# GNN and mixture-of-experts kernel on one Trainium2 core: the first expert stage finishes and normalises its own rows

## The chip, the cores and the metric

The kernel is one program on one NeuronCore of a Trainium2 chip. The metric is the device time of one execution in microseconds (us), the median of three runs. TensorE (PE in the profile; PEld is its weight loading), VectorE (DVE), ScalarE (ACT), GpSimd (POOL) and SyncE (SP) each run their own instruction stream. They meet only in semaphores. All transfers are issued by SP, ACT or POOL and run on the core's 16 DMA engines.

## The reference

The input is a graph of 3125 nodes with 256 features and 53125 edges. Two layers follow one another, each a graph part and a feed-forward part with experts. Around the change stands this:

```python
x = x + _L0_gnn_ref(_layernorm(x), ...)                  # attention over the edges
x = x + _L0_ffn_ref(_layernorm(x)[None], ...)[0]         # one of 8 experts a node
#   H = gelu(xf @ W1 + b1); probs = softmax(H @ Wg + bg); e = argmax(probs)
#   out = probs[e] * (H @ Wd[e] + bd[e])
x = x + _L1_gnn_ref(_layernorm(x), W1, W2, b, src, dst)
#   feat = _layernorm(x); out_deg = how often a node is a source, at least 1
#   msg = (feat @ W1)[src] + (feat[src] * feat[dst]) @ W2
#   msg = msg / (sqrt(out_deg[src]) * sqrt(out_deg[dst])); agg = segment_sum(msg, dst)
x = x + _L1_ffn_ref(...)                                 # two of 8 experts a node
```

All sums over `src` in the second graph part are linear in `feat[src] / sqrt(out_deg[src])`. The kernel therefore gathers rows of the normalised x, scaled by the root of the degree, and calls them f.

## The kernel before, in words

The program is a row of blocks. In each block every engine has its own list of instructions, and all engines meet at the block's end. Nodes stand in T = 25 tiles of P = 125 rows, five tiles to a group (G = 5, NG = 5). `x_sb` is x in SBUF, `n_sb` the normalised x.

**Attention update (lines 1178 to 1390).** For each group VectorE adds the projected attention to `x_sb`, normalises it and keeps it in `n_sb`. SP stores `x_sb` to the DRAM tensor `sum0` (line 1205) and `n_sb` to `tok0` (line 1208). VectorE also works out `rsq_deg`, the inverse root of the out-degree (line 1265), after the first group.

**Routing `route("r0", ...)`.** Every node picks one expert; nodes are sorted into NB0 = 32 blocks of S = 128 rows, each of one expert. `from_i`, `to_i` and `gate_i` hold, column by column, the node rows that a block reads, the rows that it writes (unfilled slots go to 256 spare rows behind the nodes) and its gate values.

**First expert stage `experts("m0", ...)`.** All 32 blocks pass through it in turns of two slots. The second expert stage `m1` (56 blocks) uses the same function with `own_w1` true.
- SP: `load_w2` waits for `s_ye`, then loads the block's 1 MB second weight (line 1660) and its bias (line 1661), into one of two slots.
- POOL: for block b it issues `load_rows(b + 3)`, an indirect gather of 128 rows from `tok0` (line 1678); `add_rows(b)`, which waits for the finished rows and for the store before and then scatters them into `sum0` with an add on the way (line 1693); and `load_gates(b + 2)` (line 1684).
- PE, in a loop over turns: hidden(b + 1), 32 matmuls (line 1739); turn(b + 2), two transposes (line 1728); output(b), 16 matmuls (line 1762).
- ACT: the gelu of the hidden values.
- DVE, for block b: `fetch_rows` copies the turned rows of block b + 2 from PSUM (line 1805), which the hidden product of that block waits for. Then `fetch_output(b)` waits for the output, adds the bias (line 1819), releases `s_ye`, waits for the gate and multiplies by it (line 1823).

`dve_order.link` (line 62 in the trace) makes an instruction raise a semaphore on which the next one of the same engine waits. In a loop each such wait takes its value from a register, for which a small register instruction is issued. `v.sem_inc(carrier, 1)` carries one wait more.

**Load, normalise, store (lines 1849 to 1935).** After the experts: SP loads all of `sum0` into `x_sb` (line 1904); VectorE takes mean and variance of each row (lines 1870, 1873), an inverse root by a shift and three Newton steps (`inverse_root`, lines 162 to 167, eleven instructions), and ScalarE (line 1895) and VectorE (line 1886) write f into `yt`; SP stores it to `f_rows` (line 1908) and waits for the store.

**Edge sums (lines 1940 to 2116).** For 84 groups of 5 edge columns, POOL gathers the rows f[src] from `f_rows`, 381 gathers (line 1969; it runs up to GI = 4 groups ahead of VectorE). 39 more columns are made by TensorE instead (line 1989), from one-hot matrices (line 2015) and `f_part`, f split into three bf16 parts; for these SP first loads f back in five chunks (line 2110). VectorE adds up runs (line 2027), ACT keeps the sums (line 2099), SP stores them (line 2115). In groups 3 to 27 VectorE also writes one tile of `n_sb` each (line 2052), for the stage behind.

Of the kernel before, what the change touches and what calls it, by code (L numbers as in the profile page):

```python
# [8 lines left out]
ALU = mybir.AluOpType  # L9
# [62 lines left out]
def build(nc, x, src, dst, edge_attr_64, L0_gnn_Wq, L0_gnn_Wk, L0_gnn_Wv, L0_gnn_We, L0_gnn_Wo, L0_gnn_bo,  # L72
# [22 lines left out]
    with top:  # L95
# [8 lines left out]
        f_rows = dram("f_rows", [N_NODES, D])  # L104
# [4 lines left out]
        sum0 = dram("sum0", [N_NODES + 2 * S, D])  # L109
# [1070 lines left out]
        s_lgT, s_res, s_fold = sem2("logits_turned"), sem2("residual_ready"), sem2("fold_made")  # L1180
        s_tok = [sem(f"tokens{n}_stored") for n in range(2)]
        s_base = [sem(f"residual{n}_stored") for n in range(2)]
        HALF = (313, 312)
        with ExitStack() as st:
# [13 lines left out]
            @block.sync  # L1198
            def _(sp):
                for n, rows in enumerate((sum0, sum1)):  # L1200
                    sp.dma_start(rows[N_NODES:N_NODES + 2 * S], x[0:2 * S]).then_inc(s_base[n], 16)
                with sp.Fori(0, NG) as i:
                    sp.wait_ge(s_kept3, i + 1)
                    for a, b in HALVES:
                        sp.dma_start(rows_of_tiles(sum0[0:N_NODES])[a:b, bass.ds(i * G, G), :], x_sb[a:b, bass.ds(i * G, G), :])\
# [14 lines left out]
            def _(v):  # L1220
# [44 lines left out]
                inverse_root(v, rsq_deg[:], degree[:], root_t[:, 0:T])  # L1265
                for i in range(2, NG):
# [125 lines left out]
        v_ctx.close()  # L1392

# [219 lines left out]

        def experts(name, n_blocks, tok, s_tok, total, s_base, W1, W2, b2, own_w1):
# [8 lines left out]
            with ExitStack() as st:  # L1623
# [7 lines left out]
                yr = [sb(st, f"{name}yr_{n}", [S, D]) for n in range(2)]  # L1631
# [6 lines left out]
                s_yg, s_gate = sem(name + "_y_weighed"), [sem(f"{name}_gate{n}_loaded") for n in range(2)]  # L1638
                block = st.enter_context(nc.Block(no_gpsimd_drain=True))
# [34 lines left out]
                def _(pool):  # L1674
# [12 lines left out]

                    def add_rows(b):
# [12 lines left out]
                    pool.wait_ge(s_base, 32 * NG + 16)  # L1701
                    for b in range(n_blocks):
# [86 lines left out]
                def _(v):  # L1789
# [34 lines left out]

                    v.sem_inc(s_ye, 2)
                    for s in range(2):
                        fetch_rows(0, s, slice(s, s + 1))
                    for s in range(2):
                        fetch_rows(1, s, slice(s + 2, s + 3))
                        fetch_output(0, s, slot_used=False)  # L1830
                    with v.Fori(1, turns - 1) as t:
                        dve_order.turn(t - 1, 4 if own_w1 else 2)
                        for s in range(2):
                            fetch_rows(t + 1, s, bass.ds(t * 2 + s + 2, 1))
                            fetch_output(t, s)
                    dve_order.leave(turns - 2)
                    for s in range(2):
                        fetch_output(turns - 1, s)
# [4 lines left out]
        experts("m0", NB0, tok0, s_tok[0], sum0, s_base[0], L0_ffn_W1, L0_ffn_Wd, L0_ffn_bd, False)  # L1843
# [5 lines left out]
        s_mv6, s_f6, s_f6d, s_f6st = sem("moments6_ready"), sem("f6_ready"), sem("f6_last_ready"), sem("f6_stored")  # L1849
        n6_ctx = ExitStack()  # L1850
        mv6 = sb(n6_ctx, "mv6", [P, T, 2])
        inv_dev6 = sb(n6_ctx, "inv_dev6", [P, T])
        with ExitStack() as st:
            yt = sb(st, "yt6", [P, T, D])
            stats6 = sb(st, "stats6", [P, T, 6])
            sq6 = sb(st, "sq6", [P, T])
            scale6 = sb(st, "scale6", [P, T])
            shift6 = sb(st, "shift6", [P, T])
            block = st.enter_context(nc.Block(no_gpsimd_drain=True))
            PARTS6 = (slice(0, 3), slice(3, NG))  # L1860

            @block.vector
            def _(v):
                link = lambda ins: dve_order.link(v, ins)

                def moments(i):

                    v.wait_ge(s_sum[i], 32)
                    for t in range(i * G, (i + 1) * G):
                        last = nc.vector.bn_stats(stats6[:, t, :], x_sb[:, t, :])  # L1870
                    link(last)
                    for t in range(i * G, (i + 1) * G):
                        last = nc.vector.bn_aggr(mv6[:, t, :], stats6[:, t, :])
                    link(last)

                for part in PARTS6:
                    for i in range(part.start, part.stop):
                        moments(i)
                    tiles = slice(part.start * G, part.stop * G)
                    link(nc.vector.tensor_scalar(sq6[:, tiles], mv6[:, tiles, 1], LN_EPS, None, ALU.add))  # L1880
                    inverse_root(v, inv_dev6[:, tiles], sq6[:, tiles], root_t[:, tiles])
                    link(nc.vector.tensor_tensor(scale6[:, tiles], inv_dev6[:, tiles], rsq_deg[:, tiles], ALU.mult))
                    nc.vector.scalar_tensor_tensor(shift6[:, tiles], mv6[:, tiles, 0], -1.0, scale6[:, tiles], ALU.mult, ALU.mult)\
                      .then_inc(s_mv6, 1)
                for t in range((NG - 1) * G, T):
                    last = nc.vector.tensor_scalar(yt[:, t, :], x_sb[:, t, :], mv6[:, t, 0:1], scale6[:, t:t + 1],
# [605 lines left out]
```

## Time and profile before

| | us |
|---|---|
| median of 3 runs | 2324.05 |
| lowest and highest | 2320.11, 2327.67 |
| the profiled execution's own time | 2315.66 |
| its span, first to last instruction | 2313.9 |

| stage | from, to in the profiled span (us) |
|---|---|
| attention update | about 734, 875 |
| routing | 875, 926 |
| first expert stage | 926, 1175 |
| load, normalise, store | 1175, 1207 |
| edge sums | 1207, 1697 |
| second graph part, routing | 1697, 1876 |
| second expert stage, output | 1876, 2314 |

In the profile, busy times are sums over a whole run or a window. "Idle before <-releaser" is how long the engine stood before an instruction, and what ended it. A DMA's "us to landing" runs from the issue's start to its semaphore.

### The profile page before, as it was taken

The numbers are of one execution on the slowest core, as the hardware profiler recorded it, in microseconds if no ns is written. First come the engines' busy times: TensorE is split into PE (matmuls) and PEld (weight loads), VectorE is DVE, ScalarE is ACT, GpSimd is POOL, SyncE is SP. The second block draws the span as 40 slices with busy tenths as digits, with TensorE's granted clock in tenths as the row PEclk, the third lists the DMA queues.
The fourth block names the chain that finished last, engine by engine and source line by source line (L and its number), as shares of the span: only waits on it lengthen the run. The fifth ranks groups of instructions, "written<-read, shape, count | busy, mean of one in ns | idle before, by whom it ended". The sixth has DMA issues, their size and how long they took to land. (4 is left out here: it accounts for less than half of the span.)

```text
span 2313.9 us, 39305 instructions
## 1 busy us (share of the span) xinstructions
PE 1788.1 (77%) x12108; PEld 1523.0 (66%) x12109; DVE 1236.2 (53%) x2537; ACT 909.2 (39%) x1928; POOL 1179.8 (51%) x1175
## 2 busy tenths in 40 slices
PE   5627987878864896899912888788868459999996
PEld 4415766666654674899912777677647459999996
DVE  6527977777778532111137887777737742222221
ACT  4415765555531343344424222222224243333442
POOL 1575777777741200444417777777750024444443
PEclk9858987787776898899965998989979569999998
DMA  5387655555564110676767766666640467777775
GB/s 124 100 186 170 171 155 154 154 155 155 152 155 100 46 45 23 191 199 199 200 167 208 237 219 219 219 220 230 223 143 23 143 211 198 198 198 196 198 199 147
DMA packets 224088, 383.62 MB, mean 166 GB/s; under 512 B 38181, under 2 KB 167748, under 8 KB 223764
## 3 DMA queue, kind: packets, MB, share of 16 engines
q1 hardware_dynamic: 158988, 243.83, 34.6%
q0 software_dynamic: 64160, 136.38, 23.4%
q10 hardware_dynamic: 840, 2.16, 0.3%
q8 instruction: 52, 0.85, 0.2%
q14 instruction: 48, 0.39, 0.1%
HBM read 287.62 MB, written 98.35 MB: 167 GB/s over the span
## 5 line engine op out<-in xcount | busy, mean ns | idle before, releaser
L790 POOL DMA_INDIRECT qr<-q_rows,src_t x405 | 396.2, 978 | 140.3 <-issue 120.3
L1969 POOL DMA_INDIRECT fr<-f_rows,src_i x381 | 360.6, 946 | 155.1 <-issue 112.7
L1989 PE MATMUL psP<-f_part,onehot 125*128 125x256 bf16 x2925 | 359.3, 287 | 80.3 <-DVE onehot L2015 80.3
L1989 PEld LDWEIGHTS psP<-f_part,onehot 125*128 125x128 bf16 x2925 | 298.2, 103 | 134.7 <-DVE onehot L2015 88.1
L884 PE MATMUL psK<-kp,oh_k 126*128 x1680 | 285.0, 327 | 92.0 <-DVE qr L967 55.2
L884 PEld LDWEIGHTS psK<-kp,oh_k 126*128 126x128 bf16 x1680 | 189.8, 113 | 182.5 <-issue 107.4
L2027 DVE SCALAR_TENSOR_TENSOR psA<-psA,same,fr 128x256 f32<-128x256 f32 x420 | 206.5, 492 | 89.7 <-DMA fr<-f_rows,src_i 57.7
L2099 ACT ACTIVATE acc<-psA 128x1280 f32<-128x1280 f32 x84 | 103.9, 1237 | 327.5 <-DVEq L2030 318.4
L1719 ACT ACTIVATE m1hT<-m1psH,m1par 128x128 f32<-128x128 f32 x448 | 128.1, 368 | 250.2 <-PE m1psH L1739 250.2
L1739 PEld LDWEIGHTS m1psH<-m1xT,m1w 128*128 128x128 f32 x1792 | 210.7, 193 | 2.8
L1739 PE MATMUL m1psH<-m1xT,m1w 128*128 128x128 f32 x1792 | 210.9, 276 | 0.0
L1762 PE MATMUL m1psY<-w_all,m1hT 128*128 x896 | 203.4, 380 | 0.0
L967 DVE TENSOR_TENSOR qr<-qr,psK 128x512 f32<-128x512 f32 (+1 forms) x252 | 136.1, 592 | 103.9 <-DMA qr<-q_rows,src_t 101.8
L1693 POOL DMA_INDIRECT sum<-m1yr,to_i x56 | 89.6, 1600 | 188.0 <-DVE m1yr L1823 185.1
L1762 PEld LDWEIGHTS m1psY<-w_all,m1hT 128*128 128x128 f32 x896 | 165.9, 190 | 21.2
L811 ACT ACTIVATE dist<-loc,k_neg 126x640 bf16<-126x640 bf16 x170 | 130.8, 819 | 67.2 <-DMA loc<-locals_ 38.5
L2015 DVE TENSOR_TENSOR onehot<-psP,node_f 125x3200 bf16<-125x3200 f32 x39 | 136.1, 3489 | 10.0 <-PE psP L1980 6.8
L1719 ACT ACTIVATE m0hT<-m0psH,b 128x128 f32<-128x128 f32 x256 | 73.2, 369 | 142.2 <-PE m0psH L1739 142.2
L970 DVE TENSOR_REDUCE dots<-qr 128x40 f32<-128x1280 f32 x84 | 125.0, 1488 | 2.9
L1739 PEld LDWEIGHTS m0psH<-m0xT,m0w 128*128 128x128 f32 x1024 | 120.6, 194 | 1.6
L1739 PE MATMUL m0psH<-m0xT,m0w 128*128 128x128 f32 x1024 | 120.7, 277 | 0.0
L815 ACT ACTIVATE oh_k<-dist,ones 126x1280 bf16<-126x1280 bf16 x85 | 115.8, 1362 | 10.1
(479 smaller groups left out, 2678.3 us busy)
## 6 DMA issues: line engine op xcount, KB each, us to landing
m1w<-in_L_ffn_W_dram SPq DMA_DIRECT2D x56, 1024.0 KB
run_rows<-acc SPq DMA_DIRECT2D x84, 640.0 KB
m0w<-in_L_ffn_Wd_dram SPq DMA_DIRECT2D x32, 1024.0 KB, 5.4
loc<-locals_ SPq DMA_DIRECT2D x85, 157.5 KB
ea<-in_edge_attr_dram SPq DMA_DIRECT2D x84, 140.0 KB
w_all<-in_L_ffn_W_dram SPq DMA_DIRECT2D x8, 1024.0 KB
m1b<-in_L_ffn_b_dram SPq DMA_DIRECT2D x56, 128.0 KB, 2.9
qr<-q_rows,src_t POOLq DMA_INDIRECT x420
```

Of the source, the lines that this page charges most:

```text
L790: nc.gpsimd.indirect_dma_start(out=qr[:, n % GQ, u, :], out_offset=None, in_=q_rows, in_offset=bass.IndirectOffsetOnAxis(ap=src_t[:, n, u: ...
L811: last = nc.scalar.activation(dist[:, c - CD, :], loc[:, slot, :], ACT.Abs, bias=k_neg[:, c:c + 1])
L884: last = nc.tensor.matmul(psK[:, m, (u - a) * D:(u - a + 1) * D], oh_k[:, K_SLOT[g], c, u * E:(u + 1) * E], kp[:, bass.ds(first[u] + c, 1) ...
L967: nc.vector.tensor_tensor(row[:, a:b].rearrange("p u d -> p (u d)"), row[:, a:b].rearrange("p u d -> p (u d)"), psK[:, m, 0:(b - a) * D], ...
L970: nc.vector.tensor_reduce(dots[:, :, at].rearrange("p h u -> p u h"), row.rearrange("p u (h d) -> p u h d", h=H), AX.X, ALU.add).then_inc( ...
L1719: last = nc.scalar.activation(hT[s][:, m, :], psH[s][:, m * 128:(m + 1) * 128], ACT.Gelu, bias=par[s][:, m:m + 1] if own_w1 else b1_0[:, m ...
L1739: last = nc.tensor.matmul(psH[s][:, m * 128:(m + 1) * 128], w1[s if own_w1 else 0][:, k, m * 128:(m + 1) * 128], xT[s][:, k, :], start=(k ...
L1762: last = nc.tensor.matmul(psY[:, s, 0:D], hT[s][:, m, :], w, start=(m == 0), stop=(m == KC - 1))
L1969: nc.gpsimd.indirect_dma_start(out=fr[:, n % GI, u, :], out_offset=None, in_=f_rows, in_offset=bass.IndirectOffsetOnAxis(ap=src_i[:, n * G ...
L1989: last = nc.tensor.matmul(psP[:, k % 2, 0:D], onehot[:, k % 2, t, :], f_part[:, c, t, :], start=(t == 0 and c == 0), stop=(t == T - 1 and ...
L2015: nc.vector.tensor_tensor(onehot[:, k % 2], psP[0:P, k % 2, D:D + E].unsqueeze(1).to_broadcast([P, T, E]), node_f[:].unsqueeze(2).to_broad ...
L2027: link(nc.vector.scalar_tensor_tensor(sums(n, u), prev, same[:, n * G + u:n * G + u + 1], fr[:, n % GI, u, :], ALU.mult, ALU.add))
```

## The change

Each block of the first expert stage now also gathers its residual rows, with the degree's root as a 257th column, from `base0`. VectorE finishes x, normalises it, scales it, and POOL scatters x and f side by side as 2 KB rows to `pair_rows`, without an add. The block that loaded, normalised and stored is gone. The edge sums gather f from `pair_rows` at index 2*src + 1 (`f_at`), load x behind group 12, take its moments in groups 24 to 48 and write `n_sb` in groups 50 to 74. In the attention update `base0` takes the place of `sum0`, and one more store writes its last column.

```diff
-        f_rows = dram("f_rows", [N_NODES, D])
-        sum0 = dram("sum0", [N_NODES + 2 * S, D])
+        base0 = dram("base0", [N_NODES, D + 1])
+        pair_rows = dram("pair_rows", [N_NODES + 2 * S, 2 * D])
...
-                for n, rows in enumerate((sum0, sum1)):
-                    sp.dma_start(rows[N_NODES:N_NODES + 2 * S], x[0:2 * S]).then_inc(s_base[n], 16)
+                sp.dma_start(sum1[N_NODES:N_NODES + 2 * S], x[0:2 * S]).then_inc(s_base[1], 16)
+                sp.wait_ge(s_root3, 1)
+                sp.dma_start(rows_of_tiles(base0[:, D:D + 1]), rsq_deg[:].unsqueeze(2), allow_slow_non_contiguous=True).then_inc(s_base[0], 16)
...
+                    def load_base(b):
+                        if b >= 2:
+                            pool.wait_ge(s_yst[b % 2], 16 * (b // 2))
+                        nc.gpsimd.indirect_dma_start(out=yr[b % 2][:, 0:D + 1], out_offset=None, in_=base0,
+                                                     in_offset=bass.IndirectOffsetOnAxis(ap=from_i[:, b:b + 1], axis=0))\
+                          .then_inc(s_xb[b % 2], 16)
+                    def store_pairs(b):
+                        pool.wait_ge(s_yg, b + 1)
+                        nc.gpsimd.indirect_dma_start(out=total, out_offset=bass.IndirectOffsetOnAxis(ap=to_i[:, b:b + 1], axis=0),
+                                                     in_=yr[b % 2][:], in_offset=None).then_inc(s_yst[b % 2], 16)
...
                         if b + 3 < n_blocks:
                             load_rows(b + 3)
-                        add_rows(b)
+                        if own_w1:
+                            add_rows(b)
+                        else:
+                            if b + 1 < n_blocks:
+                                load_base(b + 1)
+                            store_pairs(b)
                         if b + 2 < n_blocks:
                             load_gates(b + 2)
...
+                    def finish_rows(t, s):
+                        b = t * 2 + s
+                        link = lambda ins: dve_order.link(v, ins)
+                        rows, mean, var = yr[s][:, 0:D], y_mean[:, 0:1], y_root[:, 0:1]
+                        v.wait_ge(s_y, b + 1)
+                        v.sem_inc(carrier, 1)
+                        link(nc.vector.tensor_tensor(y_own[:], psY[:, s, 0:D], b2r[s][:], ALU.add))
+                        v.sem_inc(s_ye, 1)
+                        v.wait_ge(s_gate[s], (t + 1) * 16)
+                        v.sem_inc(carrier, 1)
+                        v.wait_ge(s_xb[s], (t + 1) * 16)
+                        v.sem_inc(carrier, 1)
+                        link(nc.vector.scalar_tensor_tensor(rows, y_own[:], gate_s[s][:, 0:1], rows, ALU.mult, ALU.add))
+                        v.sem_inc(carrier, 1)
+                        link(nc.vector.bn_stats(y_stats[:], rows))
+                        v.sem_inc(carrier, 1)
+                        link(nc.vector.bn_aggr(y_mean[:], y_stats[:]))
+                        link(nc.vector.tensor_scalar(var, y_mean[:, 1:2], LN_EPS, None, ALU.add))
+                        inverse_root(v, y_root[:, 1:2], var, y_root[:, 2:3])
+                        link(nc.vector.tensor_tensor(y_root[:, 1:2], y_root[:, 1:2], yr[s][:, D:D + 1], ALU.mult))
+                        nc.vector.tensor_scalar(yr[s][:, D:2 * D], rows, mean, y_root[:, 1:2], ALU.subtract, ALU.mult).then_inc(s_yg, 1)
...
-        with ExitStack() as st:
-            yt = sb(st, "yt6", [P, T, D])
...
-                sp.wait_ge(s_f6st, 32 * NG)
+        f_rows = pair_rows.rearrange("n (a d) -> (n a) d", a=2)
...
+        MOMENTS = 24
+        NORMS = MOMENTS + T + 1
...
-                    if 3 <= n < 3 + T:
-                        t = n - 3
+                    if MOMENTS <= n < MOMENTS + T:
+                        t = n - MOMENTS
+                        if t % G == 0:
+                            v.wait_ge(s_sum[t // G], 32)
+                            v.sem_inc(carrier, 1)
+                        link(nc.vector.bn_stats(stats6[:, t, :], x_sb[:, t, :]))
+                        link(nc.vector.bn_aggr(mv6[:, t, :], stats6[:, t, :]))
+                    if n == MOMENTS + T:
+                        link(nc.vector.tensor_scalar(var6[:], mv6[:, :, 1], LN_EPS, None, ALU.add))
+                        inverse_root(v, inv_dev6[:], var6[:], root_t[:, 0:T])
+                        link(nc.vector.tensor_tensor(inv_dev6[:], inv_dev6[:], has_in[:], ALU.mult))
+                    if NORMS <= n < NORMS + T:
+                        t = n - NORMS
...
                 for n in range(NK):
+                    if n >= MOMENTS // 2 and n % 2 == 0 and (n - MOMENTS // 2) // 2 < NG:
+                        i = (n - MOMENTS // 2) // 2
+                        for a, b in HALVES:
+                            sp.dma_start(x_sb[a:b, i * G:(i + 1) * G, :], rows_of_tiles(pair_rows[0:N_NODES, 0:D])[a:b, i * G:(i + 1) * G, :])\
+                              .then_inc(s_sum[i], 16)
```

## Rows read from the trace of the kernel before

**Rows 1.** The page's first line.
```profile
span 2313.9 us, 39305 instructions
```
**Rows 2.** Busy time by window, its length first; last the granted clock, DMA share, GB/s.
```profile
926.00:1171.00 245.00, 234.13 (x1600) 220.17 (x1600) 38.49 (x96) 93.78 (x272) 111.58 (x96) 0.97 0.68 192
1171.00:1207.00 36.00, 0.00 (x0) 0.00 (x0) 17.27 (x83) 9.93 (x20) 1.42 (x1) 0.50 0.72 182
1250.00:1688.00 438.00, 361.05 (x2999) 306.52 (x3000) 337.44 (x461) 116.05 (x154) 331.38 (x351) 0.91 0.68 226
```
**Rows 3.** Timeline at the end of the expert stage: start, us, engine, line, operation.
```profile
1164.92 0.42 DVE L1819 TENSOR_TENSOR m0yr<-m0psY,m0b 128x256 f32<-128x256 f32 x1 [5.99 <-PE m0psY L1762]
...
1168.37 0.42 DVE L1819 TENSOR_TENSOR m0yr<-m0psY,m0b 128x256 f32<-128x256 f32 x1 [2.42 <-PE m0psY L1762]
...
1170.87 1.56 POOL L1693 DMA_INDIRECT sum<-m0yr,to_i  x1 [3.05 <-DMA sum<-m0yr,to_i]
1175.12 6.95 SPq L1904 DMA_DIRECT2D x_sb<-sum  x10
...
1207.00 16.01 SPq L2110 DMA_DIRECT2D f_chunk<-f_rows  x10
...
1207.68 1.02 POOL L1969 DMA_INDIRECT fr<-f_rows,src_i  x1 [35.26 <-POOLq L1853]
```
**Rows 4.** Groups of POOL in the edge sums, 1250 to 1688: busy, mean, idle before.
```profile
L1969 POOL DMA_INDIRECT fr<-f_rows,src_i x351 | 332.1, 946 | 111.1 <-issue 103.9 <-DVEq L2031 7.2
```
**Rows 5.** Timelines of DVE, SP, POOL and PE over one expert block, 1049 to 1057.
```profile
1049.22 0.42 DVE L1819 TENSOR_TENSOR m0yr<-m0psY,m0b 128x256 f32<-128x256 f32 x1 [3.14 <-PE m0psY L1762]
1049.98 0.35 DVE L1823 TENSOR_SCALAR m0yr<-m0yr,m0gate 128x256 f32<-128x256 f32 x1 [0.34 <-DVE m0yr L1819]
1049.87 0.39 SPq L1660 DMA_DIRECT2D m0w<-in_L_ffn_Wd_dram  x1
1052.53 0.99 POOL L1684 DMA_INDIRECT m0gate<-gate_rows,gate_i  x1 [0.30 <-issue]
1053.82 0.96 POOL L1678 DMA_INDIRECT m0xr<-tok,from_i  x1 [0.30 <-issue]
1048.91 3.73 PE L1739 MATMUL m0psH<-m0xT,m0w 128*128 128x128 f32 x32
1056.15 3.73 PE L1739 MATMUL m0psH<-m0xT,m0w 128*128 128x128 f32 x32
```
**Rows 6.** DMA queues: packets, MB, share; in 1050.6 to 1054.4, then 1055.0 to 1056.6.
```profile
q1 hardware_dynamic: 901, 0.92, 81.3%
...
q0 software_dynamic: 215, 0.26, 77.0%
```
**Rows 7.** DVE timeline, chain of small instructions in the attention update.
```profile
784.51 0.45 DVE L177 BATCH_NORM_AGGREGATE mean_var<-stats 125x2 f32<-125x6 f32 x5 [0.15 <-DVE stats L173]
861.56 0.17 DVE L179 TENSOR_SCALAR variance<-mean_var 125x5 f32<-125x5 f32 x1
863.99 1.71 DVE L182 TENSOR_SCALAR tile_n<-x_sb,mean_var,rstd 125x256 f32<-125x256 f32 x5
```
**Rows 8.** Lines with fastest, median, slowest ns: statistics, multiply-add, link register step, wide scatter.
```profile
L1870 DVE BATCH_NORM_STATS2 stats<-x_sb x25: 406/409/427, 1180.2 to 1194.0; 125x6 f32<-125x256 f32 x25
L2232 DVE SCALAR_TENSOR_TENSOR x_sb<-gr,inv_len,x_sb x25: 475/479/485, 1772.2 to 1813.5; 125x256 f32<-125x256 f32 x25
L62 DVEq ALU_OP  x14: 40/40/40, 969.5 to 1157.9; - x14
L385 POOL DMA_INDIRECT k_rows<-k,pos_i x25: 1173/1180/2442, 86.5 to 124.2; - x25
```
**Rows 9.** DMA landings, us, minimum/median/maximum: scatters L1693, gathers L1678, scatters of 1.5 KB rows L385.
```profile
DMA to landing us min/median/max: 3.8/5.8/6.2
...
DMA to landing us min/median/max: 3.1/3.3/6.3
...
DMA to landing us min/median/max: 4.1/4.6/5.6
```

More of the change, by code:

```diff
@@ L1204, in _ @@
                     for a, b in HALVES:
[L1205 removed]
+                        sp.dma_start(rows_of_tiles(base0[:, 0:D])[a:b, bass.ds(i * G, G), :], x_sb[a:b, bass.ds(i * G, G), :])\
                           .then_inc(s_base[0], 16)
@@ L1630, in experts @@
                 hT = [sb(st, f"{name}hT_{n}", [128, KC, S]) for n in range(2)]
-                yr = [sb(st, f"{name}yr_{n}", [S, D]) for n in range(2)]
+                yr = [sb(st, f"{name}yr_{n}", [S, D if own_w1 else 2 * D]) for n in range(2)]
+                y_own = None if own_w1 else sb(st, f"{name}y_own", [S, D])
+                y_stats = None if own_w1 else sb(st, f"{name}y_stats", [S, 6])
+                y_mean = None if own_w1 else sb(st, f"{name}y_mean", [S, 2])
+                y_root = None if own_w1 else sb(st, f"{name}y_root", [S, 3])
                 par = [sb(st, f"{name}par_{n}", [128, KC + 2 * KD]) for n in range(2)]
@@ L1638, in experts @@
                 s_yg, s_gate = sem(name + "_y_weighed"), [sem(f"{name}_gate{n}_loaded") for n in range(2)]
+                s_xb = None if own_w1 else [sem(f"{name}_base{n}_loaded") for n in range(2)]
                 block = st.enter_context(nc.Block(no_gpsimd_drain=True))
@@ L1701, in _ @@
                     pool.wait_ge(s_base, 32 * NG + 16)
+                    if not own_w1:
+                        load_base(0)
                     for b in range(n_blocks):
@@ L1823, in fetch_output @@
                         nc.vector.tensor_scalar(yr[s][:], yr[s][:], gate_s[s][:, 0:1], None, ALU.mult).then_inc(s_yg, 1)
+                    def finish_rows(t, s):
[19 more added lines that the diff above has]
+                        nc.vector.tensor_scalar(yr[s][:, D:2 * D], rows, mean, y_root[:, 1:2], ALU.subtract, ALU.mult).then_inc(s_yg, 1)
                     v.sem_inc(s_ye, 2)
+                    if not own_w1:
+                        nc.vector.tensor_scalar(f_at[:], src_i[:], 2.0, 1.0, ALU.mult, ALU.add)
                     for s in range(2):
@@ L1853, in build @@
-        with ExitStack() as st:
-            yt = sb(st, "yt6", [P, T, D])
[L1855 to L1886, printed above, removed]
-                                                   ALU.subtract, ALU.mult)
-                last.then_inc(s_f6d, 1)
-            @block.scalar
-            def _(act):
-                for i in range(NG - 1):
-                    act.wait_ge(s_mv6, 1 if i < PARTS6[0].stop else 2)
-                    for t in range(i * G, (i + 1) * G):
-                        last = nc.scalar.activation(yt[:, t, :], x_sb[:, t, :], ACT.Identity, bias=shift6[:, t:t + 1],
-                                                    scale=scale6[:, t:t + 1])
-                    last.then_inc(s_f6, 1)
-            @block.sync
-            def _(sp):
-                for i in range(NG):
-                    tiles = slice(i * G, (i + 1) * G)
-                    for a, b in HALVES:
-                        sp.dma_start(x_sb[a:b, tiles, :], rows_of_tiles(sum0[0:N_NODES])[a:b, tiles, :]).then_inc(s_sum[i], 16)
-                def store_f(i):
-                    for a, b in HALVES:
-                        sp.dma_start(rows_of_tiles(f_rows)[a:b, i * G:(i + 1) * G, :], yt[a:b, i * G:(i + 1) * G, :])\
-                          .then_inc(s_f6st, 16)
-                for i in range(PARTS6[0].stop):
-                    sp.wait_ge(s_f6, i + 1)
-                    store_f(i)
-                sp.wait_ge(s_f6d, 1)
-                store_f(NG - 1)
-                sp.wait_ge(s_f6, NG - 1)
-                store_f(NG - 2)
-                sp.wait_ge(s_f6st, 32 * NG)
```

36 lines of the change are left out of this document (25 added, 11 removed).

## The prediction

> **What bounds the kernel now.** The span is 2313.9 us [rows 1]; the profiled execution's own time is 2315.66, the median of the runs 2324.05. I read the windows first, because the engines take turns at being the limit. In the first expert stage TensorE is busy 234.1 of 245 us at a granted clock of 0.97, VectorE 38.5, POOL 111.6 [rows 2]: TensorE bounds it, and a block takes 7.24 us, from one hidden product at 1048.91 to the next at 1056.15 [rows 5]. In the 36 us behind it TensorE does nothing, and no engine is busy for half of the time [rows 2]: this is load, wait, compute, wait, store, wait. In the edge sums POOL sets the pace: 351 gathers of 946 ns, each with a gap of 0.3 us that nothing outside POOL causes (103.9 of 111.1 us of its idle time is "issue"), so 1.25 us each without a break, while VectorE still has about 100 of 438 us free [rows 2, 4]. So a gather that starts x earlier ends the edge sums x earlier, and everything behind moves with it, since the block's end is a meeting of all engines.
>
> **What is removed.** The timeline at the seam shows the term. The last output leaves TensorE and its bias add starts at 1168.37; the first gather of the edge sums is issued at 1207.68 [rows 3]. That is 39.3 us, all of it on the path.
>
> **What takes its place on that path.** First the chain of `finish_rows`, added up instruction by instruction:
> - bias add 0.42 [rows 5];
> - gap to the multiply-add: before, 0.34 with two semaphore instructions between [rows 5], now there are three. I take 0.42 (bounds 0.34 and 0.5);
> - multiply-add 0.48, statistics 0.41 [rows 8], a gap of 0.15 behind each of them [rows 7];
> - aggregation, one instead of five in 0.45, so 0.09 to 0.17 and a short gap [rows 7]: I take 0.20;
> - 13 instructions on one column (the epsilon, eleven of `inverse_root`, the product with the degree's root). The trace has 12 such steps from 861.56 to 863.99, 0.20 each [rows 7]: 2.63;
> - the last tensor_scalar, 256 wide: 0.35 to 0.42 [rows 5], I take 0.41.
>
> Together 0.42 + 0.42 + 0.48 + 0.15 + 0.41 + 0.15 + 0.20 + 2.63 + 0.41 = 5.3 us (4.9 with the low values). In the loop each link has a register step of 0.04 [rows 8]. It is issued while the linked instruction, at least 0.17, still runs, so I count it as nothing. Without that cover 17 of them cost 0.7; doubled, for what surrounds such a step, 1.4: upper bound 6.7.
>
> At the end of the stage the last two outputs come 3.45 us apart, at 1164.92 and 1168.37 [rows 3]. The chain is longer than that, so the two run back to back: 1164.92 + 2 x 5.3 = 1175.5. POOL picks up 0.3 later. The scatter has landed 3.8 (the last add, alone on the queues) to 4.6 us (rows of 1.5 KB) after its issue [rows 9]; I take 4.1, at 1179.9. From a landing to the next block's first instruction the old seam took 1170.87 + 3.8 = 1174.7 to 1175.12, and from SP's first transfer to POOL's first gather another 0.68 [rows 3]: 1181.0. The old seam ended at 1207.68, so 26.7 us are gained; with all low values 28, with 6.7 for the chain and 5.6 for the landing 22.
>
> **In the expert stage, block by block.** This is where the gain could be lost 30 times over, so each resource is set against 7.24 us.
> - *VectorE.* The add is at 0 (1049.22); the chain ends at 5.3, the copy of the turned rows (0.42, and about 0.2 of waits) at 5.9. TensorE wants them at 1056.15, 6.9 after the add [rows 5]. Slack 1.0, cost nothing; with the upper bound 0.4 too late, 12 us in 30 blocks. `s_ye` still rises at the first add, so the weight loads do not move.
> - *POOL.* Rows 0.95, gates 0.98, the scatter 1.18 to 1.6 without its add [rows 5, 8, 9], base rows 0.95 to 1.2, gaps 4 x 0.3: 5.3 to 5.9. It fits.
> - *DMA.* The weight load is issued 0.65 after the add. From 1.4 to 5.2 after it q1 alone moves data (81.3% of all engines, no packet of q0); q0 is served at 77.0% only from 1055.0, 5.8 after the add [rows 6]. The base gather of block b + 1 is issued about 2.4 after block b's add, inside that burst, so it is served at its end. The gather that was issued at 1053.82 landed in 3.3 [rows 5, 9], at 7.9. VectorE wants the base rows at 7.24 + 0.84 = 8.1. Before, an accumulating scatter stood in front; it is now issued 5.6 after the add and finds the queues free until the next burst at 8.6. So the base row is in time by 0.2 to 1.0, and 1.0 more is covered by the copy's slack. Cost nothing.
>
> Here the Trainium skill speaks otherwise (DMA: Bandwidth & Descriptors, Queues, rings and completion order): each DMA engine goes round-robin between the queues that have work. By that the base gather would land some 3.3 after its issue and never late. The trace does not show it, and I keep the waiting; the sum is the same by both, the rule would only strike out the slower rival.
>
> **The rest.** The column store to `base0` is 3125 pieces of 4 bytes, and the rows beside it have a pitch of 1028 bytes. They go out in the attention update, which ends at 875, and the stage that reads them begins at 926 [rows 2], so even 50 us more would be hidden. In the edge sums VectorE gains 25 x (0.41 + 0.17 + gaps) = 16 us and one chain of 2.9 in groups 24 to 49, so 1.3 in a pair of groups, against 100 us free in 39 pairs, 2.6 each [rows 2]; POOL runs up to four groups ahead and hides it. The reload of x, five pieces, is spread over ten groups. The 25 writes of `n_sb` only move. I take 0 for all this, bounds -2 and +6.
>
> **Sum.** 2315.66 - 26.7 = 2289.0 for an execution like the profiled one; it lies 8.4 under the median, so on the median's footing 2324.05 - 26.7 = 2297.4.
>
> **Rivals.**
> - *A, slower: the loop over POOL.* Scatter of block b, base gather of b + 2 behind its landing, multiply-add behind that, scatter of b + 2. Per two blocks it needs L(scatter) + L(gather) + 4.5 of chain + 0.4 of pick-up, and 14.5 is free. With medians, 4.6 + 3.3, it has 1.7 to spare; with the slowest landings, 6.2 + 6.3 [rows 9], 17.4, so 1.45 a block too much, 43 us in 30 blocks: 2297 + 43 = 2340. It decides from 11.4 of summed landings on, where the 27 us are gone. For it: such landings occur under bursts. Against it: the scatter falls into the gap, and only the gather meets a burst. Chance 0.12.
> - *B: VectorE's chain overruns* 6.3 us in the loop, so that TensorE waits for the copy. At the upper bound 0.4 a block, 12 us, with 1.4 more at the seam twice: 2297 + 15 = 2312. Against it: nothing in the trace shows a link's register step. Chance 0.08.
> - *C: the edge sums give something back* (statistics, reload, gathers from 2 KB pitch): +6, 2303. Chance 0.08.
> - *D: POOL is held up by VectorE* while it writes descriptors, at worst one 0.4 us instruction for each of its four issues: 5.9 + 1.6 = 7.5 against 7.24, 0.3 a block, 8 us: 2305. In the edge sums, with VectorE busy three quarters of the time, a gather's mean is 946 as everywhere [rows 2, 4], so 0.03. It is the rule of the Trainium skill (SBUF — State Buffer) that a VectorE instruction in a two-port mode locks GpSimd out of a shared port; this trace does not bear it out.
>
> **Numbers.** Forecast 0.69, A 0.12, B 0.08, C 0.08, D 0.03. About 0.3%, 7 us, is what a measurement of this kernel tells from no change. B, C and D stay faster but for 0.01; of A two thirds end slower, the rest near nothing. Faster 0.87, same 0.05, slower 0.08. The range takes in the low seam (28), the spread of the runs (4 each way), C, D and B's bound: 2290 to 2314; A's tail is left out.
>
> **What would show it.** Right: TensorE's period stays 7.24; base gathers land before the add's end plus 0.4; the chain takes 5.3; first gather of the edge sums near 1181; 1.25 us per gather as before. Wrong: the multiply-add's idle time released by the base rows' DMA, or the hidden product's by the copy; a stage longer than 245 us by more than 10.

## The result and the profile after

The changed kernel takes 2374.02 us (median of 4 runs, 2369.17 to 2380.68), against 2325.86 for the kernel before, timed beside it (2320.11 to 2331.23). The ratio is 1.022, 95% interval 1.0202 to 1.0239: 48 us slower, where 26.7 us faster was forecast. The profiled execution took 2376.64.

Where did it go? Cut both traces at the same events, each stage from a first start to a last end:

| stretch (us, profiled executions) | before | after | difference |
|---|---|---|---|
| start to first hidden product of the expert stage | 935.3 | 940.3 | +5.0 |
| **first hidden product to last output** | 232.9 | 309.3 | **+76.4** |
| **last output to first gather of the edge sums** | 39.5 | 11.2 | **-28.3** |
| first to last gather of the edge sums | 480.4 | 480.7 | +0.3 |
| second graph part, to the first gather of the second expert stage | 186.7 | 188.0 | +1.3 |
| second expert stage | 419.7 | 426.2 | +6.5 |
| rest, in and around the span | 21.1 | 20.9 | -0.2 |

The sum is +61.0, the difference of these two executions. The two bold stretches, where the change works, come to +48.1; the medians differ by 48.2. The other 12.9 lie in the other rows, and part of them is the spread between executions: the profiled execution of the kernel before lies 10.2 under its median, that of the kernel after 2.6 above. The seam is the third row, from the last output of the experts to the first gather of the edge sums. The seam did what the prediction said (26.7 forecast, 28.3 found). The loss is in the expert stage.

The windows of the kernel after, to be held against [rows 2] (length, busy time of PE, PEld, DVE, ACT, POOL, granted clock, DMA share, GB/s):

```profile
940.30:1249.60 309.30, 257.27 (x1597) 233.98 (x1596) 133.79 (x582) 92.45 (x271) 117.59 (x123) 0.93 0.53 169
1249.60:1260.80 11.20, 0.02 (x1) 0.00 (x0) 5.85 (x29) 0.43 (x3) 1.99 (x3) 0.67 0.15 54
1303.00:1741.00 438.00, 361.11 (x2990) 304.67 (x2991) 355.13 (x525) 115.78 (x154) 331.37 (x351) 0.92 0.71 233
```

The same stage of the kernel before, cut at the same events:

```profile
935.30:1168.20 232.90, 232.90 (x1597) 219.36 (x1596) 37.29 (x93) 92.49 (x271) 108.03 (x92) 0.99 0.67 190
```

Before, TensorE was busy for all of 232.90 us. After, it is idle for 309.3 - 257.3 = 52 us, and its busy time is 24.4 us longer for the same work, at a clock of 0.93 instead of 0.99. So 76.4 = 52.0 idle + 24.4 of slower matmuls. No other engine is near its limit: VectorE has 134 and POOL 118 of 309 us. Something waits. The waits of the kernel after, 926 to 1300 (total, times, longest):

```profile
POOL pair_rows L1710 <- DVE m0yr L1878: 169.1, 32, 12.3
PEld m0psT L1760 <- DMA m0xr<-tok,from_i: 66.4, 16, 9.8
PE m0psT L1760 <- DMA m0xr<-tok,from_i: 63.2, 16, 9.7
```

The same of the kernel before, 926 to 1171:

```profile
POOL sum L1693 <- DVE m0yr L1823: 106.2, 31, 10.9
PE m0psT L1728 <- DMA m0xr<-tok,from_i: 10.6, 2, 9.1
```

TensorE now waits 16 times for the **rows' gather**, a part that the change does not touch. In the timeline two of these waits (9.7 and 1.5) come before the first hidden product, as the two of the kernel before do. The other 14 are 3.3 to 4.4 us each, one at every second block from 966 on, and add up to 52.0: all of TensorE's idle time. The first lines say what has changed on the queue that issues this gather: POOL stands 169 us before the scatter, where it stood 106. One such place in the timeline of the kernel after:

```profile
1050.89 0.42 DVE L1864 TENSOR_TENSOR m0y_own<-m0psY,m0b 128x256 f32<-128x256 f32 x1 [4.59 <-PE m0psY L1794]
1055.71 0.41 DVE L1878 TENSOR_SCALAR m0yr<-m0yr,m0y_mean,m0y_root 128x256 f32<-128x256 f32 x1
1056.40 0.98 POOL L1710 DMA_INDIRECT pair_rows<-m0yr,to_i  x1 [8.28 <-DVE m0yr L1878]
1057.68 0.97 POOL L1695 DMA_INDIRECT m0gate<-gate_rows,gate_i  x1 [0.30 <-issue]
1058.79 0.38 SPq L1671 DMA_DIRECT2D m0w<-in_L_ffn_Wd_dram  x1
1058.95 0.95 POOL L1689 DMA_INDIRECT m0xr<-tok,from_i  x1 [0.30 <-issue]
1064.99 0.44 PE L1760 MATMUL m0psT<-ident,m0xr 128*128 128x128 f32 x2 [3.43 <-DMA m0xr<-tok,from_i]
1065.28 5.40 PE L1794 MATMUL m0psY<-m0w,m0hT 128*128 128x256 f32 x16
```

Read it as a chain. Bias add at 1050.89; 5.2 us later VectorE's last step ends (1056.12); POOL issues the scatter at 1056.40, the gates, and only then the rows of the block four further on, at 1058.95: 8.06 us after the add, where before it was 4.6 (1049.22 to 1053.82, [rows 5]). TensorE was ready for these rows at 1064.99 - 3.43 = 1061.56, which is 10.7 us after the add. The 16 matmuls of the output behind the wait take 5.40 us instead of 3.62.

The gather also goes out 0.16 us behind the weight load. The DMA queues of the kernel after, 1060.1 to 1063.9 and then 1064 to 1066 (packets, MB, share), have the picture of [rows 6]:

```profile
q1 hardware_dynamic: 1147, 1.14, 93.3%
q0 software_dynamic: 29, 0.10, 7.0%
...
q0 software_dynamic: 140, 0.41, 53.0%
```

While the weights come in, q0, on which all gathers run, gets 29 packets, none of them between 1061 and 1063, where q1 moves 715. The rows arrive behind the weights, just before 1064.99; the rest of q0's 140 packets belongs to the scatter issued at 1063.56. The landings of the rows' gather in the kernel after, beside 3.1/3.3/6.3 before [rows 9]:

```profile
DMA to landing us min/median/max: 2.7/5.9/7.0
```

### The profile page after: what moved, and what is told of

Its sections match the earlier page's. It is cut to its first block and busy times, and to the rows that moved or that the text cites. A ratio compares the mean times of both kernels' runs of the same rounds, so it can differ in the third digit from the quotient of the medians.

```text
span 2374.9 us, 40268 instructions
## 1 busy us (share of the span) xinstructions
PE 1822.9 (77%) x12108; PEld 1541.8 (65%) x12109; DVE 1337.5 (56%) x3029; ACT 899.1 (38%) x1908; POOL 1190.3 (50%) x1207
## 5 line engine op out<-in xcount | busy, mean ns | idle before, releaser
L1970 POOL DMA_INDIRECT fr<-pair_rows,dst_i x381 | 360.5, 946 | 123.1 <-issue 113.3
L1794 PE MATMUL m0psY<-m0w,m0hT 128*128 128x256 f32 x512 | 136.4, 427 | 0.0
L1794 PEld LDWEIGHTS m0psY<-m0w,m0hT 128*128 128x128 f32 x512 | 108.5, 217 | 18.7 <-DMA m0b<-in_L_ffn_bd_dram 0.3
```

The costliest lines, as they stand in the source:

```text
L1794: last = nc.tensor.matmul(psY[:, s, 0:D], hT[s][:, m, :], w, start=(m == 0), stop=(m == KC - 1))
L1970: nc.gpsimd.indirect_dma_start(out=fr[:, n % GI, u, :], out_offset=None, in_=f_rows, in_offset=bass.IndirectOffsetOnAxis(ap=f_at[:, n * G ...
```

## The experiments

Three theories. **Q, queue order:** `load_rows` of the next iteration stands on POOL behind the scatter, which waits for the 5 us chain; so it is issued too late, and into the weight burst. **D, data crowding:** the new transfers (base rows in, 2 KB rows out) crowd the rows' gather wherever it is issued. **V, the chain itself:** VectorE's long chain holds TensorE up directly, by the copy of the turned rows or the bias add. The runs were made on several chips. On two of them the kernel before takes 2674 and 2700 us, because other stages are slower there; the first expert stage takes nearly the same time on all (the changed kernel 309.3 and 313.2 us on two chips, the version with the rows first 234.1 to 236.4 on three). So the stage is compared in us, from first hidden product to last output, and totals only with the kernel before on the same chip.

**Rows first.** The changed kernel, the rows' gather issued one block further ahead, so before the scatter of its block:

```diff
-                    for b in range(3):
+                    ahead_by = 4 if not own_w1 else 3
+                    for b in range(ahead_by):
                         load_rows(b)
...
-                        if b + 3 < n_blocks:
-                            load_rows(b + 3)
+                        if b + ahead_by < n_blocks:
+                            load_rows(b + ahead_by)
```

> The changed kernel with one edit: in the first expert stage POOL issues the row gather of block b + 4 ahead of block b's scatter, instead of the row gather of b + 3 ahead of it (which in time is that of b + 4 behind block b's scatter). Three theories. Q, the queue: the row gather stands on POOL behind a scatter that waits for VectorE's chain of 5 us, and so comes into the weight burst; with this edit TensorE never waits for rows, the first expert stage falls from 309 to about 233 us between its first hidden product and its last output, and the kernel comes to 2374 - 76 = about 2298. D, the data: the base gather and the 2 KB scatter crowd the DMA engines; then nothing changes, 2374. V, VectorE: its chain is too long for the 7.24 us of a block; then also nothing changes, 2374.

Measured: 2640.86 us against 2674.04 before on that chip, ratio 0.987 (0.9828 to 0.9909). The stage takes 235.5 us. The two waits for rows that are left are those ahead of the first hidden product. The line of its window:

```profile
1121.90:1357.40 235.50, 233.46 (x1597) 219.21 (x1596) 133.88 (x584) 90.80 (x271) 118.79 (x123) 0.99 0.70 223
```

and of its waits (total, times, longest):

```profile
PE m0psT L1761 <- DMA m0xr<-tok,from_i: 10.6, 2, 8.6
```

VectorE does the same 134 us of work and POOL the same 119; nothing of the change was taken out. The 76 us are gone, and the clock is back at 0.99. The timeline shows the gather still going out beside the weight load, 0.08 behind it:

```profile
1235.84 0.42 DVE L1865 TENSOR_TENSOR m0y_own<-m0psY,m0b 128x256 f32<-128x256 f32 x1 [1.70 <-issue]
1236.49 0.39 SPq L1671 DMA_DIRECT2D m0w<-in_L_ffn_Wd_dram  x1
1236.57 0.95 POOL L1689 DMA_INDIRECT m0xr<-tok,from_i  x1 [0.30 <-issue]
```

But these rows are wanted a block later. That speaks for Q and against V (same chain). Against D it says less: a landing that new transfers had made late would be covered by the extra block too. The next run takes these transfers away.

**The chain alone.** The kernel before with 16 more linked VectorE instructions (the expectation says 15) between bias add and scatter, results unused; no base rows, no pairs:

```diff
                         v.sem_inc(carrier, 1)
+                        if not own_w1:
...
+                            link(nc.vector.tensor_scalar(y_own[:], yr[s][:], gate_s[s][:, 0:1], None, ALU.mult))
...
+                            link(nc.vector.bn_stats(y_stats[:], y_own[:]))
...
+                            link(nc.vector.bn_aggr(y_mean[:], y_stats[:]))
+                            link(nc.vector.tensor_scalar(y_root[:, 0:1], y_mean[:, 1:2], LN_EPS, None, ALU.add))
+                            inverse_root(v, y_root[:, 1:2], y_root[:, 0:1], y_root[:, 2:3])
+                            link(nc.vector.tensor_tensor(y_root[:, 1:2], y_root[:, 1:2], y_root[:, 1:2], ALU.mult))
                         nc.vector.tensor_scalar(yr[s][:], yr[s][:], gate_s[s][:, 0:1], None, ALU.mult).then_inc(s_yg, 1)
```

> The kernel before with VectorE's chain alone: statistics, inverse root and a product on scratch tiles between the bias add and the gate product, 15 linked instructions whose results nobody reads. No base gather, no wider scatter, the seam stage still there. Q: the scatter is issued some 4.5 us later, the row gather behind it falls into the weight burst, and the stage takes about 76 us more: 2325 + 76 = about 2400. D: no new data, so 2325 within 7. V: as Q or less; e1 tells these two apart.

Measured: 2763.83 us (one run; before 2674.04 on that chip), 90 us more. The stage takes 316.1 us, and the waits are like those of the changed kernel: 14 in the loop, 3.5 to 5.8 us each. The line of the window:

```profile
1122.20:1438.30 316.10, 259.17 (x1597) 235.49 (x1596) 129.03 (x586) 92.22 (x271) 105.91 (x90) 0.92 0.53 141
```

and of its waits (total, times, longest):

```profile
PE m0psT L1732 <- DMA m0xr<-tok,from_i: 67.2, 16, 8.4
```

So the longer wait of POOL for VectorE is enough for the whole loss, without one byte of the new transfers. D is out.

**Chain and order together**, the fourth corner: the kernel just above with the rows' gather moved as in the first experiment.

> The kernel before with the chain of small VectorE instructions alone and the rows' gather one block further ahead in the first expert stage, nothing else of the change: the fourth corner of the square (neither, chain alone, order alone, both). Queue order (Q): the chain then costs the stage nothing, 233 to 237 us from the first hidden product to the last output in place of 316 with the chain alone, no wait for rows in the loop, 16 matmuls of an output in 3.62 us throughout. Long chain by itself (V): it stays above 290.

Measured: 2329.36 us (one run) against 2325.87 before on that chip; the stage takes 234.7 us. The line of its window:

```profile
940.20:1174.90 234.70, 233.21 (x1598) 219.29 (x1596) 130.17 (x589) 92.48 (x271) 107.13 (x91) 0.99 0.71 189
```

and of its waits (total, times, longest):

```profile
PE m0psT L1733 <- DMA m0xr<-tok,from_i: 10.7, 2, 8.5
```

The square, in us for the stage: neither 232.9, order alone 233.8 (below), chain alone 316.1, both 234.7. The four come from three chips, and those with the chain are single runs; against the 4 us by which the changed kernel's stage differs between chips, 83 is no matter of chance. The chain costs 83 us in one order and 1 in the other. V is out too: with the chain in place and the rows first, TensorE has no wait in the loop.

**A shorter chain.** The changed kernel with two Newton steps of three in `finish_rows`, then with one: 0.6 and 1.2 us off the chain, order untouched.

```diff
-        def inverse_root(v, y, a, t):
+        def inverse_root(v, y, a, t, steps=3):
...
-            for _ in range(3):
+            for _ in range(steps):
...
-        FINISH_LINKS = 17
+        FINISH_LINKS = 14
...
-                        inverse_root(v, y_root[:, 1:2], var, y_root[:, 2:3])
+                        inverse_root(v, y_root[:, 1:2], var, y_root[:, 2:3], 2)
```

> The changed kernel with two Newton steps instead of three in each block's inverse root, a chain 0.6 us shorter. Q with the cliff: the row gather's descriptors are ready at about 8.6, when the burst starts, so some blocks escape and some do not: between 2300 and 2374, and TensorE's waits for rows are either about 3.9 us long or absent, few between. Q without a cliff: each wait 0.6 shorter, about 2362. D: 2374. V: 2374 - 19 = 2355.

> The changed kernel with one Newton step instead of three in each block's inverse root (the normalised rows are less exact), so a chain shorter by six instructions or 1.2 us, nothing else. Q with a burst that shuts the software queue out: the row gather is issued about 7.0 us after the bias add, has its descriptors at about 8.0, just ahead of the burst that starts at 8.6, and TensorE's wait vanishes: about 2300. Q without such a cliff: TensorE's wait of 3.9 us on every second block shrinks by 1.2 to 2.7, 20 to 25 us less, about 2350. D: 2374. V: a chain 1.2 shorter would give at most 1.2 a block, 2374 - 38 = 2336.

Measured, with two steps, 2662.65 us (one run; before 2674.04 on that chip), the window:

```profile
1118.90:1387.10 268.20, 240.96 (x1597) 222.41 (x1596) 119.80 (x494) 91.62 (x271) 117.44 (x123) 0.98 0.63 196
```

and of its waits (total, times, longest):

```profile
PE m0psT L1760 <- DMA m0xr<-tok,from_i: 37.8, 16, 9.1
```

With one step, 2648.47 us (one run, same chip), the window:

```profile
1120.50:1363.00 242.50, 236.06 (x1597) 220.47 (x1596) 105.98 (x403) 89.82 (x271) 118.81 (x122) 0.99 0.70 217
```

and of its waits (total, times, longest):

```profile
PE m0psT L1760 <- DMA m0xr<-tok,from_i: 16.1, 7, 8.1
```

309, 268, 242 us for three, two, one (the first on another chip; 313 on a third): the first 0.6 us off the chain bring back 41 us. Of these 25 are idle time of TensorE (52.0 to 27.2) and 16 slower matmuls that are gone (257.3 to 241.0). The 14 waits of the loop fall from 3.7 to 1.9 us in the mean, so by 1.8 for the 0.6: the delay is not passed on one to one. The expectation was waits that are whole (3.9) or absent; they are neither, but 1.0 to 3.3 us at every second block. With one step five are left in the loop, of 0.8 to 1.8. A place in the run with two steps:

```profile
1223.25 0.95 POOL L1689 DMA_INDIRECT m0xr<-tok,from_i  x1 [0.30 <-issue]
1223.67 0.38 SPq L1671 DMA_DIRECT2D m0w<-in_L_ffn_Wd_dram  x1
1228.28 0.44 PE L1760 MATMUL m0psT<-ident,m0xr 128*128 128x128 f32 x2 [1.84 <-DMA m0xr<-tok,from_i]
1228.56 3.72 PE L1794 MATMUL m0psY<-m0w,m0hT 128*128 128x256 f32 x16
```

Issued 0.42 ahead of the weight load, the rows are used 5.0 us later; issued 0.16 behind it, in the changed kernel, 6.0. With one step a gather goes out at 1223.20, 1.08 ahead of the load at 1224.28, and is used at 1226.88 without a wait, so it took at most 3.7. The place against the burst sets how long the gather takes, and does so steeply.

**Small weights.** How much of it is the burst? The changed kernel with an eighth of each second weight loaded in the loop; the rest stays as it was for the first expert, from a load ahead of the loop:

```diff
+                        sp.wait_ge(s_w1c, 16)
+                        for s in range(2):
+                            sp.dma_start(w2[s][:], W2[0:1].rearrange(...)).then_inc(s_w1c, 16)
+                        sp.wait_ge(s_w1c, 48)
...
-sp.dma_start(w2[s][:], W2[bass.ds(e, 1)].rearrange(...)).then_inc(s_w2[s], 16)
+sp.dma_start(w2[s][:, 0:1, :], W2[bass.ds(e, 1), 0:128].rearrange(...)).then_inc(s_w2[s], 16)
```

> The changed kernel, in which a block of the first expert stage loads one of the eight parts of its second weight (128 KB in place of 1 MB); the other seven parts are left as they were for the first expert, so this part of the computation is not done. The rows' gather is still issued behind the scatter, 8.2 us after the bias add, but meets no burst. Q with the burst as its second half: the gather lands in 3 us instead of 5.9, at 11.2 to 11.5 where TensorE wants it at 10.9; waits of up to 0.6 us at every second block, 10 us in all instead of 63, and a stage of 233 to 250 us. If the place behind the scatter were enough by itself, the stage would stay above 290.

Measured: 2698.92 us (one run; before 2699.73 on that chip). The stage takes 265.1 us; the waits are more than halved, not gone. The line of its window:

```profile
1146.50:1411.60 265.10, 240.69 (x1596) 222.06 (x1596) 133.65 (x581) 91.93 (x271) 118.90 (x124) 0.98 0.33 99
```

and of its waits (total, times, longest):

```profile
PE m0psT L1764 <- DMA m0xr<-tok,from_i: 27.9, 15, 8.0
```

A gather issued at 1272.03 is used at 1276.35:

```profile
1272.03 0.94 POOL L1693 DMA_INDIRECT m0xr<-tok,from_i  x1 [0.30 <-issue]
1276.35 0.44 PE L1764 MATMUL m0psT<-ident,m0xr 128*128 128x128 f32 x2 [1.71 <-DMA m0xr<-tok,from_i]
```

4.3 us, not the 3.0 that I expected, so my 233 to 250 missed. Part of the miss is the experiment's own doing: its load ahead of the loop holds the first output up, so that the first bias add comes 19.9 us after the first hidden product, where it was 12.3. From the first bias add to the last output the stage takes 245.2 us, against 297.0 in the changed kernel and 220.4 in the kernel before. So of 76.6 us there, 24.8 are left. Without the start the mean wait is (27.9 - 8.0) / 14 = 1.4 us, against 52.0 / 14 = 3.7 in the changed kernel. The seven eighths of the burst that are gone thus make 2.3 of the 3.7. The other 1.4 are not those of an empty queue: q1 still moves 0.26 MB beside this gather (an eighth of the weight and the bias). In the loop the outputs behind these waits take 3.72 us, near their old 3.62, where behind 12 of the 14 waits of the changed kernel they take 5.02 to 5.40.

**The changed kernel again, rows first in both stages, and the order alone in the kernel before**, on one chip:

> The changed kernel itself, unaltered, so that it and the versions with the rows' gather first are timed on one chip. All theories: the first expert stage takes 305 to 312 us from the first hidden product to the last output, with 16 waits of TensorE for the rows' gather; the seam from the last output to the first gather of the edge sums 11 us; the ratio to the kernel before 1.015 to 1.025 (it was 1.022).

> The changed kernel with the rows' gather one block further ahead, so before the scatter of its block, in both expert stages. Queue order (Q): the first stage as when only it was changed, 233 to 238 us and no wait for rows in the loop; in the second stage the waits for rows (13 to 17 us in some ten places) go too, so 8 to 17 us less than with the first stage alone: ratio to before about 0.980 where the first stage alone has 0.986. Data crowding (D): in the second stage the gather is crowded by weight loads of 1 MB and 1 MB a block wherever it is issued, so the waits stay and the ratio is that of the first stage alone, 0.984 to 0.989.

> The kernel before with the same order in both expert stages and nothing else of the change. It separates what the order gives by itself from what the change gives with it. Q: the first stage has hardly a wait for rows to lose, so it stays within 2 us of its 233; the second stage loses its waits, 5 to 14 us; ratio 0.994 to 0.999. If the order gave the whole gain of the changed version, the ratio would be 0.98, and the seam would count for nothing.

| one chip, us | median | ratio to before | stage 1 | seam | stage 2 (first to last output product) |
|---|---|---|---|---|---|
| before | 2699.73 | | | | |
| after | 2747.90 | 1.018 (1.0137 to 1.0219) | 313.2 | 11.1 | 407.0 |
| after, rows first in both | 2663.07 | 0.988 (0.9837 to 0.9916) | 236.4 | 10.7 | 398.0 |
| before, rows first in both | 2690.82 | 0.997 (0.9947 to 0.9990) | 233.8 | 40.1 | 398.1 |

The first stage of the unaltered kernel, 313.2, lies 1.2 above the range that was expected for it. The order alone gives 9 us in the kernel before. In the changed kernel the second stage gets 9.0 us shorter (7.6 from its first hidden product, 415.6 to 408.0), and its waits for rows fall from 16.4 us in 9 places to 11.0 in 2, the start. That is the low edge of Q's 8 to 17 us, and the waits account for 5.4 of it. The ratio, 0.988, is not Q's 0.980 but lies in the range given for D: I had put the 10 us of the start, which nothing removes, into the sum, and compared ratios from two chips. That the waits of the loop go tells the theories apart here, the ratio doesn't. Between the two versions with the same order lie 2690.82 - 2663.07 = 27.8 us, with a spread of some 20 us between the executions of each: that is what the change is worth once the rows go first. The prediction's 26.7 was this number.

**The better version once more**, on a chip where the kernel before takes what it took at first:

> The changed kernel with the rows' gather one block further ahead in both expert stages, once more, for a second comparison with the kernel before. Ratio 0.985 to 0.990 (0.9876 the first time); first expert stage 234 to 238 us, seam 10.5 to 11.5, and if the chip is one on which the kernel before takes some 2325 us, 2293 to 2300: 2325 less 28 for the seam and some 3 for the second stage, plus 3 for the first.

Measured: **2292.81 us** (2292.07 to 2295.89) against 2325.87, ratio 0.986 (0.9839 to 0.9880): faster than both kernels, and 0.2 under the 2293 to 2300 expected. Stage 234.1, seam 11.2. The rows' gathers still land late here, after 3.8/6.2/7.9 us (minimum, median, maximum), and in the loop nothing waits for them:

```profile
942.20:1176.30 234.10, 234.10 (x1598) 220.32 (x1596) 133.51 (x582) 92.48 (x271) 118.95 (x123) 0.99 0.69 223
```

## Why the prediction was wrong

**The step that failed** is the item POOL in "block by block": it added up POOL's busy time, found 5.3 to 5.9 of 7.24 us, and said "It fits". As a sum that was near enough (4 issues with their gaps measured 5.0), but it is no answer. A queue that is half idle can still issue too late. The step had to name what stands behind the scatter's wait, and by the code in the change that is the gates and `load_rows(b + 3)` of the next iteration. All the rows for it were there; its own base gather "about 2.4 after block b's add" puts the rows' gather ahead of it at 1.2, which is 8.4 after the add before. Chain 5.3, pick-up 0.3, scatter 1.18 [rows 8], gates 0.98 [rows 5], two gaps of 0.3 [rows 4]: issued 8.4 after the add, measured 8.06. With the landing of 3.3 [rows 9] that is 11.7, and issued beside the weights, which shut q0 out until 5.8 after the next add by the prediction's own reading [rows 6], it is 7.24 + 5.8 = 13.0 or more; TensorE turns them behind its hidden product, at 1056.15 + 3.73 - 1049.22 = 10.7 after the add [rows 5]. So 1.0 to 2.3 us late or more, with nothing to cover it; measured 3.3 to 4.4, at every second block (a wait gives the gather behind it the time that it lacks: the one issued at 1045.92 is used at 1054.15, without a wait). The prediction did this very sum for the base rows, which it had just seen added, and not for the rows' gather, which was old and only moved in time. Of its signs of being wrong the last one came, a stage longer by more than 10 us; the two that name a wait did not, since neither names the rows' gather.

**The rivals.** A (a loop over POOL, 0.12, 2340 us) had the right engine and the wrong link: the base rows behind the scatter's landing. In the trace VectorE's multiply-add never waits for them; all that it waits for in 32 blocks is its own add, 13.3 us in all and at most 0.5 at once. B, C and D did not occur: the chain took 5.2, the edge sums as long as before, and the gathers 946 ns in both kernels, with VectorE busy 355 instead of 337 of 438 us. The port rule that D names, of the Trainium skill (SBUF — State Buffer, SBUF: two separate sides), no run here shows.

**The clock** was in no term. The granted clock stayed at 1.00 of 2.4 GHz while TensorE stood idle from 1041.4 to 1045.1, and fell behind it:

```profile
1041.40:1045.10 3.70, 0.00 (x0) 0.00 (x0) 1.45 (x8) 2.43 (x5) 1.42 (x2) 1.00 1.01 322
1045.60:1050.40 4.80, 4.80 (x18) 3.97 (x17) 0.42 (x1) 0.00 (x0) 1.91 (x3) 0.68 0.20 56
1050.60:1054.00 3.40, 3.40 (x32) 3.40 (x31) 2.18 (x9) 1.14 (x4) 0.00 (x0) 1.00 0.25 64
```

0.68 over 4.8 us is a mixture of the two levels, 1.2 and 2.4 GHz; the next product runs at full clock again. Over the stage the slower matmuls add 24.4 us to the 52.0 of waiting.

**What was right.**
- The seam, with its parts in the timeline of the kernel after, as in [rows 3]:

```profile
1246.13 0.42 DVE L1864 TENSOR_TENSOR m0y_own<-m0psY,m0b 128x256 f32<-128x256 f32 x1 [1.88 <-PE m0psY L1794]
1251.19 0.41 DVE L1864 TENSOR_TENSOR m0y_own<-m0psY,m0b 128x256 f32<-128x256 f32 x1
1256.96 0.98 POOL L1710 DMA_INDIRECT pair_rows<-m0yr,to_i  x1 [4.43 <-DVE m0yr L1878]
1260.10 2.37 SPq L2121 DMA_DIRECT2D f_chunk<-pair_rows  x5
1260.76 0.99 POOL L1970 DMA_INDIRECT fr<-pair_rows,dst_i  x1 [2.82 <-POOLq L1629]
```

  The two chains run back to back, as forecast: from the first add to the scatter 10.8 us, where 2 x 5.3 + 0.3 stood. From the scatter's issue to SP's first transfer it takes 3.1 us where 4.1 + 0.45 stood, which is most of the 1.6 us by which the gain came out larger.
- The chain: 5.3 forecast, 5.2 found; the scatter of 2 KB rows takes POOL 0.98 us, less than the 1.18 of its low bound. The register step of a link is hidden, at 0.19 us a link.
- The base rows are in time, the column store is hidden (issued at 779.74, in the attention update), and the edge sums keep their 1.25 us a gather:

```profile
L1970 POOL DMA_INDIRECT fr<-pair_rows,dst_i x351 | 332.0, 946 | 111.4 <-issue 104.5 <-DVEq L2032 6.9
```

**What stays open:** in this profiled pair the first expert stage begins 5.0 us later and the second takes 6.5 longer. The 5.0 need not be the change's: in "chain and order together", whose code up to there is that of the kernel before, the first hidden product starts at 940.2, as after the change (940.3). In the second stage, whose code is the same, TensorE is idle 3.9 us longer and busy 2.6 longer. Its waits for rows there vary between executions with this order (12.9 us before, 16.7 after, 14.1 in chain and order together, 13.1 with the rows first in the first stage alone), and with the rows first they come down to the start. What the 1.4 us are made of that stay with small weights, the 0.26 MB that q1 still moves or the scatter ahead on q0, was not tried.

## What to carry to other kernels

When an instruction on an in-order queue gets a wait, or its wait gets longer, list every instruction behind it on that queue, with the time at which its result is wanted; the sum of busy times says nothing about that. Transfers that are old and unchanged are the first to look at, since nobody costs them anew. Here the cure was one constant: issue the next loads ahead of the waiting store, one block earlier, and the change came out at 27.8 us, with 26.7 forecast.

## What the runs showed of the hardware that I had not expected

- A wait can cost TensorE more than its length: behind 12 of the 14 waits of 3.3 to 4.4 us in the changed kernel the 16 matmuls of an output took 5.02 to 5.40 us instead of 3.62. Behind the other two (3.7 and 3.8 us) they took 3.71 and 3.72, as behind the 14 waits of 1.2 to 1.7 us with small weights; so the length of the wait alone does not decide it.
- A small shift in issue has a large effect: 0.6 us off the chain took 41 us off the stage. Issued 0.16 us behind the 1 MB load on another queue, the gather took 6.0 us to be used; 0.42 ahead of it 5.0; 1.08 ahead at most 3.7. Behind a load of 128 KB (and the bias, as large) it took 4.3. The trace gave q0 7.0% during the 1 MB load. The Trainium skill (DMA: Bandwidth & Descriptors, Queues, rings and completion order) has each engine go round-robin between queues that have work; this trace does not agree, as little as [rows 6] did.
- Where the kernel before takes 2674 and 2700 us, the edge sums take 626 to 635 us instead of 480 in the versions run there, and the first expert stage as long as ever. There POOL also waited 131 us for VectorE's release of a buffer (in 1450 to 2040, the kernel before with rows first), and TensorE's clock was 0.81 instead of 0.91 [rows 2]. Whether the clock is the cause was not tried. The seam shrank by as much on such a chip, 40.1 to 10.7 us.
